# A prologue's placeholder matmuls and one small broadcast, cut into sixteen 32x32 tiles of TensorE

## The reference

```python
# layers 0 and 3: grouped convolution, 9 taps, 4 groups, plus a context and a bias
out = conv(x, weight, groups=4) + (c @ c_weight.T)[:, :, None] + bias[None, :, None]
# layers 1 and 2: a 1x1 convolution whose matrix is mixed per sample from 8 matrices
h = gelu(c @ W0 + b0); h = gelu(h @ W1 + b1); att = softmax(h @ W2 + b2)   # 32 x 8
out = einsum(einsum(att, weight), x) + (att @ bias_k)[:, :, None]
x = x + layer(x)          # four times: layers 0, 1, 2, 3
```

## Time and profile before

| | us |
|---|---|
| three timed runs | 661.17, 661.62, 661.68 |
| their median | 661.62 |
| span of the profiled execution | 658.9 |
| PE busy in that span | 648.5 |

### The profile page before, as it was taken

The page is one execution under the profiler, slowest core; times in us unless marked ns, Lnnn a source line. Parts: engine busy times, 40 slices in busy tenths (PEclk is TensorE's granted clock), DMA queues, the critical chain, the costliest instruction groups (busy, mean ns, idle before and its releaser), DMA issues.

```text
span 658.9 us, 24674 instructions
## 1 busy us (share of the span) xinstructions
PE 648.5 (98%) x11218; PEld 591.5 (90%) x11218; DVE 476.4 (72%) x948; ACT 263.7 (40%) x332; POOL 242.3 (37%) x87
## 2 busy tenths in 40 slices
PE   8999999999999999999999999999999999999995
PEld 6889999999999999999999999999999999999995
DVE  7997877677677677677677677677677677677635
ACT  5743423433423433423433423433423433423424
POOL 4024433442433442433442433442433442433220
PEclk9999999999999999999999999999999999999999
DMA  7355676545466545466545466545566545554425
GB/s 236 98 166 180 201 226 225 165 155 203 149 223 223 164 155 202 148 223 223 163 156 200 150 223 223 164 155 199 151 223 223 161 158 199 153 163 161 144 83 193
DMA packets 50325, 118.77 MB, mean 180 GB/s; under 512 B 5557, under 2 KB 26090, under 8 KB 42474
## 3 DMA queue, kind: packets, MB, share of 16 engines
q1 hardware_dynamic: 49026, 116.56, 54.2%
q10 hardware_dynamic: 1064, 1.61, 0.8%
q0 software_dynamic: 192, 0.02, 0.0%
HBM read 35.33 MB, written 33.55 MB: 105 GB/s over the span
## 4 chain that ended last, share of the span: by engine, by line
PE 95%; DVE 2%; DMA 1%; ACT 1%; issue 0%; DVEq 0%
PE ps L894 79%; PE ps L964 14%; PE ps L951 1%; DMA out_sb<-in_L_cond_weight 1%; PE ps L932 1%; DVE x_in L777 1%; DVE x_planes L780 0%; DVE x_hi L820 0%; DVE acc L718 0%; DVE mat L718 0%; ACT L616 0%; PE ps L1002 0%; ACT x_planes L566 0%; PE ps L944 0%; DVE taps_raw L738 0%
## 5 line engine op out<-in xcount | busy, mean ns | idle before, releaser
L417 POOL COPY out_sb<-out_planes 128x2048 f32<-128x2048 f32 x30 | 118.6, 3954 | 220.4 <-DVE mat2T L718 208.4
L408 POOL COPY x_planes<-x_in 128x2048 f32<-128x2048 f32 x29 | 112.8, 3889 | 137.4 <-DVE x_lo L665 137.4
L485 ACT ACTIVATE y_hi<-ps,bias_tab 128x512 fp32r<-128x512 f32 x128 | 77.5, 689 | 188.4 <-PE ps L894 188.4
L689 DVE SCALAR_TENSOR_TENSOR z_lo<-ps,bias_tab,z_hi 128x1024 fp32r<-128x1024 f32 x62 | 76.8, 1280 | 68.7 <-ACT z_hi L495 68.6
L679 DVE SCALAR_TENSOR_TENSOR y_lo<-ps,bias_tab,y_hi 128x512 fp32r<-128x512 f32 x128 | 87.2, 744 | 38.4 <-ACT y_hi L485 38.4
L894 PE MATMUL ps<-z_hi,taps_lo 32*128 32x512 f32 x1488 | 99.3, 397 | 0.0
L894 PE MATMUL ps<-x_lo,taps_hi 32*128 32x512 f32 x1536 | 96.6, 391 | 0.0
L894 PE MATMUL ps<-x_hi,taps_hi 32*128 32x512 f32 x1536 | 96.0, 390 | 0.1
L894 PE MATMUL ps<-x_hi,taps_lo 32*128 32x512 f32 x1536 | 96.1, 389 | 0.0
L503 ACT ACTIVATE out_taps<-ps,bias_tab 128x512 f32<-128x512 f32 x62 | 39.3, 684 | 133.9 <-PE ps L894 133.9
L894 PE MATMUL ps<-z_hi,taps_hi 32*128 32x512 f32 x1488 | 92.8, 391 | 0.0
(11 more groups left out here) (124 smaller groups left out, 553.1 us busy)
## 6 DMA issues: line engine op xcount, KB each, us to landing
x_in<-in_x SPq DMA_DIRECT2D x31, 1024.0 KB, 5.1
out_planes<-out_taps SPq DMA_DIRECT2D x122, 256.0 KB, 2.5
out<-out_sb SPq DMA_DIRECT2D x30, 1024.0 KB, 4.5
mix_w<-prod SPq DMA_DIRECT2D x126, 128.0 KB, 3.6
x_in<-in_x SPq DMA_DIRECT2D x2, 512.0 KB, 5.0
out<-x_planes SPq DMA_DIRECT2D x7, 128.0 KB, 2.7
out_taps<-in_L_cond_weight SPq DMA_DIRECT2D x1, 512.0 KB, 5.3
mix_w<-in_L_cond_weight SPq DMA_DIRECT2D x1, 512.0 KB, 6.5
```

The source lines that it names most:

```text
L408: pool.tensor_copy(x_planes[:, :, :], planes(x_in[t.par(d)], slice(0, S))).then_inc(x_planed, 1)
L417: pool.tensor_copy(out_sb[t.par(d)][:, :].rearrange("c (s p) -> c p s", p=PH), out_planes[:, :, :])\
L485: act.activation(y_hi[:, g, :], ps[:, bank(t, 0) + g, :], ACT.Identity, bias=bias_tab[:, b, g:g + 1]).then_inc(y_hi_done, 1)
L689: dve.scalar_tensor_tensor(out=z_home(t, 0)[1][:, 2 * h:2 * h + 2, 1:S + 1], in0=ps[:, k:k + 2, :], scalar=bias_tab[:, b, 2 * G:BIAS], in1 ...
```

## The change

Two places of PE's prologue change. `keep_busy(12)`, twelve float32r matmuls of 128x128 weights by 512 columns, becomes `keep_tiles_busy(4)`: four rounds of sixteen plain float32 matmuls, each with 32x32 weights by 512 columns, the same zeros read through a float32 view. The four matmuls of `spread_attention`, each of 32 rows and 128 output columns of the array, become sixteen of 32 rows and 32 columns; each of the four groups' semaphore increments stands on the group's last tile. The `keep_busy(3)` and `keep_busy(1)` after it stay.

```diff
                 for r in range(G):
-                    pe.matmul(ps[:, G + r, 384:512], ones[rows(r), :], spread[rows(r), :, :].rearrange("n m k -> n (m k)"),
-                              start=True, stop=True).then_inc(att_tab_psum, 1)
+                    for q in range(PH):
+                        last = pe.matmul(ps[rows(q), G + r, 384:512], ones[rows(r), rows(q)],
+                                         spread[rows(r), :, :].rearrange("n m k -> n (m k)"), start=True, stop=True)
+                    last.then_inc(att_tab_psum, 1)
...
+            def keep_tiles_busy(n):
+
+                zeros = y_hi[:, 0, :].bitcast(F32)
+                for _ in range(n):
+                    for g in range(G):
+                        for q in range(PH):
+                            pe.matmul(ps[rows(q), g, :], zeros[rows(g), rows(q)], zeros[rows(g), :], start=True, stop=True)
+
             zero, first = Step(0, 0), Step(0, 1)
             pe.wait_ge(zeros_done, 1)
-            keep_busy(12)
+            keep_tiles_busy(4)
```

## The result

The changed kernel takes 663.2 us in the median of 13 runs (661.83 to 663.45), the kernel before 661.65 us (661.17 to 662.51, 13 runs beside it). The ratio is 1.0016, 95% interval 1.0009 to 1.0024: 1.06 us slower (0.6 to 1.6), which lies within 0.2%. The means, 662.83 and 661.76 us, differ by as much; the medians differ by more, 1.55 us, because the changed kernel's times lie in two groups, six at 661.83 to 662.52 and seven at 663.20 to 663.45. The forecast was 662.1 us, range 661.2 to 665.0. By the ratio it stays within 0.2% and on the slower side, as forecast, but the cost is more than twice the 0.45 us of the sum, and the median of 663.2 lies above the range of the forecast proper, 661.5 to 662.8.

What follows compares the result with a forecast made beforehand. The prediction took PE to bound the sample loop, leaving only the prologue's chain to move. It added +0.3 us (spread) and +0.15 (zeros) to 661.62, giving 662.1 us, range 661.2 to 665.0 for 8 in 10.

Steps and rivals of the forecast that it cites:

- the sum: Prologue costs added up: +0.3 us for the attention's spread and +0.15 for the zeros, +0.45 us in all.
- the forecast proper: The main case, slower by the summed prologue costs: 662.1 us, its own range 661.5 to 662.8, chance 0.60.
- part on the zeros: Zero matmuls in PE's prologue: tiles end at 6.4 us, conv0 moves 0 to 0.1 us, 0.15 us put down.
- zero matmuls past 7 us, conv0 after 9.2: Signs in PE's prologue that would show the forecast wrong; expected were zeros ending near 6.4 and conv0 at 8.6 to 8.8.
- the rival of the late clock: Prologue: with tiles the clock rises later or not while they run; +2.2 us, 663.8, up to 666.5; chance 0.20.
- What bounds the kernel: Sample loop bound by PE, busy 98% of the span and untouched by the change; only the prologue's chain can move.
- The rate of a round: Sixteen zero tiles run side by side: 1.71 us a round at the lower clock level, 0.9 taken at the higher.
- D: How late the condition's transpose starts on PE after the zeros: about 6.6 instead of 6.17, so 0.4 us.
- Its worst case: Clock level stays low into conv0, so PE's prologue pieces lengthen: +4 to +5 us, up to 666.5.
- Who notices: Behind the transpose, ACT and PE have about 0.4 us to spare, so conv0 moves only by the lateness beyond 0.4.
- The spread: Attention's spread in sixteen side-by-side tiles: +0.1 us for starts, +0.2 for leaving, +0.3 us arriving whole; bounds -0.2 to +0.9.
- the way out: From the spread's tiles to the next convolution's row tiles: a mode-change gap and an unhidden weight load, 0.2 us.

Runs made afterwards that it cites:

- e2: Kernel before with only the zeros changed to four rounds of sixteen float32 tiles, spread as before: 662.79 us against 661.71, ratio 1.0015.
- e4: Kernel before with sixteen instead of twelve whole-array zero matmuls: 661.79 us, ratio 1.0003.
- e7: Kernel before with zeros as four rounds of four float32 tiles of 32 rows and 128 columns, spread as before: 661.81 us, ratio 1.0003.
- e11: Kernel before with the attention's spread in sixteen tiles and done four times over: 664.42 us against 661.51, ratio 1.0057.
- e9: Kernel before with sample 2's load issued ahead of the first mix_w transfers: 661.54 us against 661.51, ratio 1.0000.
- e1: Kernel before with only the attention's spread cut into sixteen tiles, zeros as before: 662.23 us against 661.71, ratio 1.0009.
- e8: Kernel before with 24 instead of 18 turns of sample 1's conv0 ahead of the first mix: 661.46 us against 661.68, ratio 0.9999.
- e12: Kernel before with its spread of four row tiles done four times over: 662.78 us, ratio 1.0018.
- e3: Changed kernel with two rounds of zero tiles instead of four: 667.54 us, ratio 1.0100 against the kernel before.
- e6: Kernel before with zeros as three rounds of sixteen tiles (twelve passes), spread as before: 662.31 us, ratio 1.0007.
- e10: Changed kernel with sample 2's load issued ahead of the first mix_w transfers: 662.35 us, ratio 1.0012 against the kernel before.
- e5: Kernel before with eight instead of twelve whole-array zero matmuls: 666.66 us against 661.68, ratio 1.0068.

## Why the prediction was right, and where its sum was off

The time fell into the range, and on the side forecast, with a sum that was too small by more than half. By the prediction's own signs its part on the zeros was wrong: "zero matmuls past 7 us, conv0 after 9.2" is what came (8.3 and 10.27 us). The range held 663.2 because the rival of the late clock had widened it, not because the forecast was near.

**What bounds the kernel.** Right. The loop did not change, and everything that the change costs was lost before 26 us.

**The rate of a round.** At the lower level the 1.71 us were right: the changed kernel's four rounds start at 1.32, 3.03, 4.74 and 6.44 us, so sixteen tiles do run side by side. The step "I take 0.9" for the higher level was too low. e2 and e4, with the same passes and rises 0.04 us apart, differ by 0.5 us at the transpose, and e2 loses it in its last two passes: one of 0.63 us instead of the 0.43 of e7, and a last one whose starts are spread over 0.45 us instead of 0.12. The prediction asked whether issuing could set the pace and bounded it by 30 ns a pair from the last convolution. In e11 a pair took 14.5 ns, less than that bound; what the prediction did not ask is whether the tiles stay in step. Why the pauses between their starts come is open.

**When the clock rises.** This is the step that failed in size more than any other. The sum used the 4.3 us of the one profile and D = 0.4. In the profiles of kernels with twelve whole-array matmuls ahead, the rise came at 4.30 (before), 4.60 (e11), 5.30 (e9), 5.57 (e1), 5.98 (e8) and 7.56 us (e12); with tiles at 5.23 (e3), 5.88 (e2), 5.90 (e6), 6.36 (e10) and 6.85 (changed); with sixteen whole-array matmuls at 5.84 (e4), with four row tiles at 4.90 (e7). The moment moves by over 3 us between executions of the same instructions, and 4.3 was the earliest seen. With the mean of the six kernels with twelve, 5.55, in its place the sum would have given D = 1.0 and +0.9 us in all. "Each 1 us by which the clock rises later makes the tiles end 0.5 us later" is right to 0.02 us. In the changed kernel's profile D was 8.25 - 6.17 = 2.08, 1.7 more than the 0.4 of the sum. The later rise makes (6.85 - 4.3) x 0.5 = 1.3 of it, and the 0.4 left is about what the pace of the tiles cost against the whole array (0.5). The prediction saw this edge and put only 0.15 us on it.

What it costs in the mean: conv0 starts at 8.63, 8.76, 8.77, 8.78, 8.88 and 9.08 us in the six kernels with twelve whole-array matmuls, 8.82 in the mean, and at 9.78, 10.02 and 10.27 in the three with four rounds of tiles, 10.02: 1.2 us. With the spread's 0.13 that is 1.3 us, inside the measured 0.6 to 1.6. Of the 1.2, some 0.45 is the four passes more (e4's conv0 at 9.27 against 8.82), 0.5 the form (e2 against e4), and the rest the later rises of the changed kernel and e10; with one profile for each kernel these shares are rough.

The rule cited from the Trainium skill ("TensorE: Matmul & The Clock Gate", Part 1), that the moment of the rise varies from run to run, agrees with these rises. The 500 ns either way that it gives do not: these lie over 3 us apart, and there the measurement decides.

**The rival of the late clock.** In the profile of the changed kernel it is what happened, nearly to its price: the rise came in the fourth round, the zeros ended at 8.3 us as worked out there, and D was 2.08 against 2.3. In the mean of the runs about half of its +2.2 us came. Its reason is another: rises come late with whole-array matmuls too, at 4.30 to 7.56 us against 5.23 to 6.85 with sixteen tiles. That tiles delay the rise by some tenths of a microsecond is not excluded by so few profiles. That they can't raise the clock or hold it fell with e3, where they alone raised it at 5.2 us, and with e6, where twelve passes of them held it. Its worst case, the level staying low into conv0, is what e3 and e5 show when the zeros are cut: +6.6 and +4.5 us where +4 to +5 was worked out.

**Who notices.** Right for the late ends: conv0 moved by D less 0.44 or 0.45 us in the changed kernel (2.08 - 0.44 = 1.64), e2, e4 and e10. It is not right where the level stays low beyond the zeros. In e12 the rise came at 7.56 us, D was 0.57, and conv0 was late by 0.45 and not by 0.17: PE's own steps up to conv0 took longer. So the prediction's remark that little of a late end would count with twelve matmuls at the lower level doesn't hold.

**The spread.** +0.3 was put down, 0.12 to 0.13 measured from the spread to the product. That the tiles run side by side rather than in turns was right. That the loss arrives whole was nearly right. The parts were wrong: the 0.2 for the way out isn't there as a price of its own (e11 and e12 leave nothing over that is clear of 0.03 us), and the start of the tiles costs more than 0.1, since 32 pairs take 0.46 us where eight took 0.22. Between the spread and the next convolution 0.19 are lost (0.44 - 0.25), and 0.07 of them come back before the product. The rule of the Trainium skill ("TensorEngine Tiling (Array Packing)", Key Properties) that changing the mode drains TensorE is neither shown nor refuted: the next convolution's matmuls start 0.20 us behind the last tile's instead of 0.01 behind the last row tile's, but by e11 and e12 that wait fits into what the passes themselves take.

**What was not foreseen.** The path from the first product to the first mix scatters by over 1 us between executions, and the profile of before caught the shortest of all. Here the comparison of two profiles, 2.5 us, overstated the change by 0.76 us. Why the second `mix_w` issue takes 0.6 us at one time and 1.45 at another, and the last of the four transfers 4.16 (before) or 5.49 (e6), is open: sample 2's load is not the cause (e9), and a slow issue is not needed for it, since e6 has the longest stretch of all, 7.84 us, with an issue of 0.71.

No version here beats the kernel before: e8 and e9 are level with it.

## What to carry to other kernels

Placeholder matmuls that raise the clock have two sides: too few and the clock is low when the real work comes (4.5 to 6.6 us here), too many and they stand in front of it. Eight passes were too few in both forms and twelve kept the clock up in every profile, with rises from 4.3 to 7.6 us; what lies between was not tried. So vary the number, and look at several profiles, not at one rise. Cutting a short matmul into sixteen tiles multiplies loads and starts, and here a pass took no less than its 32 pairs of load and matmul at 14.5 ns each. And where two profiles differ in a stretch that the change doesn't touch, look at more profiles of that stretch before any of it is given to the change.

## What the runs showed of the hardware

- Sixteen 32x32 float32 tiles with 512 moving columns run side by side at the lower level, 1.71 us a round in the changed kernel, but they go out of step: starts within 0.12 us in the first pass, spread over 0.45 in e2's last one, against 0.02 for four row tiles (e7).
- The rise of TensorE's clock came between 4.30 and 7.56 us in kernels whose instructions up to there are the same.
- With eight passes of zeros the clock either rose at 5.2 us and fell back at 8.6 (e3) or didn't rise before 20.3 us (e5), although PE was busy for 9.99 of the 10.1 us from 8.7 us on in e3.
- Sixteen 32x32 float32 tiles with 128 moving columns: 0.46 us a pass, 14.5 ns for a pair of weight load and matmul; four 32x128 row tiles: 0.22 us. Going from these tiles to the convolution's row tiles showed no price beyond that.
- A DMA issue on ACT's queue took 0.63 to 1.45 us for the same 128 KB, and held up the activation behind it.
